# A mixture of experts whose token rows are gathered instead of scattered, in a decoder kernel on one core

## The chip, the core and the metric

The kernel runs on one core of a Trainium2 chip. The core has a matrix engine (PE), a vector engine (DVE), a scalar engine (ACT), GpSimd (POOL) and a queue engine (SP) that mostly issues DMAs. Each runs its own list of instructions and waits on semaphores that the others raise. On-chip memory (SBUF) has 128 partitions; PE writes to PSUM, which has 8 banks. The metric is the device time of one execution in microseconds, lower is better.

## What is computed

x is 16 blocks of 128 tokens by 256 features, in float32. The decoder is six stages, each adding its result to x: two of layer 0 (a recurrent mixing, then a grouped attention), a feed-forward stage with experts, and three of layer 1 (windowed attention, cross attention, a gated feed-forward). The change is about the third, which is, cut to what matters:

```python
x = x + ffn(_layernorm(x))

def ffn(h):
    dense = _rms((_gelu_tanh(_rms(h, pre1) @ w_gate) * (_rms(h, pre1) @ w_up)) @ w_down, post1)
    probs = softmax(_rms(h) * router_scale * ROOT @ router_w)        # 8 experts
    top_w, top_i = top_k(probs, 2)
    top_w = top_w / sum(top_w) * per_expert_scale[top_i]
    moe = sum over the 2 chosen e of top_w * ((_gelu_tanh(m @ we_gate[e]) * (m @ we_up[e])) @ we_down[e])
                                             # m = _rms(h, pre2)
    return _rms(dense + _rms(moe, post2), post)
```

## The kernel before

The third stage (function `experts`, L1059 to L1830) starts when all engines have left the second (`gqa`). Its tokens are 4 groups of 4 blocks (`GB` = 4, `NG` = 4).

**The normalised tokens y.** DVE aggregates the statistics of all 16 blocks (`aggregate`, L195), POOL makes one factor per token from them (L200 to L1232, first for 4 blocks, then for 12), and DVE multiplies (`normalise`, L1591: 4 blocks, then 12).

**PE's opening.** `turn(0)` and `turn_ahead(1..3)` transpose y, 8 matmuls of 128x128 for each group (L1281, L1292); ACT copies the result to SBUF; `route(g)` multiplies it by the router's weights (L1300, 8 matmuls with 8 columns, which the trace prints as 16). `turn(0)`, `turn_ahead(1)` and `route(0)` come first, then the first dense step, `gate_up(0,0)`, and behind it the other turns and routes.

**The dense part.** Every group has 8 steps. A step is `gate_up(g,q)` (L1333, 12 matmuls of 512 columns) and, one step late, `down(g,q-1)` (L1350, 12 matmuls of 256 columns). Between the two ACT takes the gelu (L1552), DVE multiplies (`ex_gated`, L1675), ACT rounds to the high part (`ex_hidden_high`, L1559) and DVE makes the low part (L1682). `down` waits for the high part. Each operand is split in two parts, so that three matmuls make one product; the weights' low parts are made on POOL (L1237).

**Where each token goes.** Once all four routes are done, DVE reads the logits, ACT takes the exponent, and DVE ranks the experts of each token by comparing all pairs (L1606 to L1616, tiles of 128x1024). A token's two experts are the ones with rank under 2. `count()` on PE (L1308 to L1311, before `gate_up(0,4)`) counts how many tokens of each expert come before each one. From that DVE finds for each token two slots (`ex_index`) among 40 tiles of 128 slots, each tile of a single expert (`ex_owner`).

**The rows by slot.** POOL scatters the rows of y into the DRAM tensor `slot_x` by 32 indirect DMAs (L1244), which wait for the slots of all tokens. SP then fetches the 40 tiles in 20 pairs (L1181), into 4 buffers. Slots that no token fills have to hold zeros: SP writes the whole of `slot_x` in the first stage (L276, 5 MB).

**The mixture.** It comes on PE between dense groups 1 and 2 (`EARLY` = 2). A pair of tiles is turned (L1362), goes through its expert's gate and up (L1376), the hidden is turned (L1386) and goes through the expert's down (L1396). SP stores its result to `slot_y`. When all 20 pairs are stored, POOL gathers for each block the two rows of every token into `ex_first` and `ex_second` (L1220, 32 indirect DMAs). Right after the last store SP loads the fourth stage's weights wk, wv, wo (L182).

**The late work.** Beside dense groups 2 and 3 (16 steps, n = 0 to 15) and behind them, four groups of results are put together: ACT weighs `ex_first` (`weigh_first`, L1484), DVE adds the weighed `ex_second` (`mix`, L1704), ACT squares (L1468), POOL makes the norm (`normalise`, L1214 and L1215), DVE scales and adds the dense part (L1711, L1723), ACT squares again, POOL makes the norm, DVE scales (L1729), adds to x (`add_sum`, L1736) and takes the statistics (`measure`, L1741). Each group starts 4 steps behind the one before it (`late`, `late_step`, `FIRST_LATE` = 2). The fourth stage's first matmul needs the statistics of all of x.

## Time and profile before

| | us |
|---|---|
| median of 3 runs | 1493.51 (1492.75 to 1494.72) |
| the profiled execution | 1493.66, of which its span is 1491.6 |
| first stage / second stage | 0 to 205 / 205 to 343 |
| third stage | 344.4 to 646.6 |
| its dense groups 0 and 1 end, its mixture starts and ends, groups 2 and 3 end | 459.3, 480.0, 547.1, 628.2 |
| fourth, fifth and sixth stage | from 646.6 to the end |
| mean granted clock of PE | 0.936 of full speed |

Times inside the trace count from the start of the span. The row of a group of instructions gives its start, its busy time, the engine, the line, the operation, what it writes and reads, how many instructions of what shape, and in brackets how long the engine sat idle before it and who ended that.

### The profile page before, as it was taken

What the parts mean: (1) busy time and instruction counts of PE and PEld (TensorE: products, weight loads), DVE (VectorE), ACT (ScalarE), POOL (GpSimd) and SP (SyncE); (2) the same over time, 40 slices, a digit from 0 to 9 for tenths busy, and PEclk for the clock granted to TensorE, in tenths of its full rate; (3) what the DMA queues carried; (4) which work ended last, traced back from release to release, by engine and by line L of the source; (5) the groups of instructions that cost most, each with busy time, mean ns of one, the idle gap of its engine ahead of it and who ended that gap; (6) DMA issues with size and microseconds to landing.
All of it is one profiled execution on the core that took longest, in us unless ns stands there. A gap on an engine that the chain in (4) does not pass through costs nothing. (4 is left out here: it accounts for less than half of the span.)

```text
span 1491.6 us, 26479 instructions
## 1 busy us (share of the span) xinstructions
PE 1249.2 (84%) x7839; PEld 983.0 (66%) x7886; DVE 981.7 (66%) x1905; ACT 843.0 (57%) x2174; POOL 641.1 (43%) x724
## 2 busy tenths in 40 slices
PE   6994889995793999638998998899896888879998
PEld 4673555554683897526777777777774555548887
DVE  5998788883453544797778778777773566643443
ACT  5443899993452555545666666666662555543322
POOL 2003666663436015457667666666663333320000
PEclk9996999997797999958999999999998999988999
DMA  8400433310003454120000000000000000000000
GB/s 312 156 0 14 105 93 84 84 43 1 0 33 116 142 195 138 29 102 1 2 1 0 0 0 0 0 0 0 0 1 3 4 4 3 3 1 1 15 14 29
DMA packets 49684, 64.52 MB, mean 43 GB/s; under 512 B 6032, under 2 KB 42896, under 8 KB 48336
## 3 DMA queue, kind: packets, MB, share of 16 engines
q1 hardware_dynamic: 46544, 55.27, 11.8%
q0 software_dynamic: 3072, 8.39, 1.7%
q8 instruction: 37, 0.61, 0.2%
q14 instruction: 31, 0.25, 0.1%
HBM read 38.48 MB, written 16.78 MB: 37 GB/s over the span
## 5 line engine op out<-in xcount | busy, mean ns | idle before, releaser
L2209 ACT ACTIVATE wi_weights<-wi_psum,wi_bias,wi_scale 128x128 f32<-128x128 f32 x256 | 113.7, 454 | 118.2 <-DVE wi_bias L2319 118.2
L929 ACT ACTIVATE gq_weights<-gq_psum,gq_least 128x128 f32<-128x128 f32 x512 | 151.2, 524 | 2.0 <-DVE gq_least L977 2.0
L1984 POOL TENSOR_TENSOR wi_straight<-wi_straight,wi_crossed 128x512 f32<-128x512 f32 x80 | 103.3, 1291 | 10.9 <-DVE wi_crossed L2305 10.8
L977 DVE TENSOR_REDUCE gq_least<-gq_psum 128x4 f32<-128x512 f32 x128 | 86.1, 686 | 26.9 <-PE gq_psum L854 25.5
L1972 POOL TENSOR_TENSOR wi_scratch<-wi_sums,wi_eps 128x4 f32<-128x4 f32 x80 | 35.1, 438 | 132.6 <-DVE wi_sums L2288 131.2
L1973 POOL TENSOR_TENSOR wi_scale<-wi_scratch,minus_half 128x4 f32<-128x4 f32 x80 | 84.6, 1058 | 6.3
L2108 PE MATMUL wi_psum<-wi_weights_t,wi_values 128*128 128x512 f32 x128 | 68.9, 620 | 20.6 <-DVE wi_weights_t L2326 20.6
L2310 DVE TENSOR_REDUCE wi_top<-wi_psum 128x4 f32<-128x512 f32 x64 | 44.0, 687 | 63.1 <-PE wi_psum L2099 63.1
L2099 PE MATMUL wi_psum<-wi_k_t,wi_q_t 128*128 128x128 f32 x512 | 67.5, 275 | 19.8 <-ACT wi_q_t L2200 18.7
L862 PE MATMUL gq_psum<-const,gq_weights 128*128 128x128 f32 x512 | 79.1, 278 | 1.3 <-ACT gq_weights_t L937 0.3
L2735 DVE TENSOR_REDUCE cr_top<-cr_psum 128x4 f32<-128x512 f32 x64 | 43.7, 682 | 46.0 <-PE cr_psum L2550 46.0
L862 PEld LDWEIGHTS gq_psum<-const,gq_weights 128*128 128x128 f32 x512 | 63.1, 142 | 14.8 <-DVE gq_weights_t L990 4.2
L1994 POOL TENSOR_TENSOR wi_weights<-wi_weights,wi_inverse 128x512 f32<-128x512 f32 x64 | 66.2, 1034 | 9.5 <-remote 5.1
L2099 PEld LDWEIGHTS wi_psum<-wi_k_t,wi_q_t 128*128 128x128 f32 x512 | 67.9, 193 | 1.6
L2050 PEld LDWEIGHTS wi_psum<-const,wi_straight 128*128 128x128 f32 x320 | 39.6, 143 | 42.7 <-issue 41.8
L2490 POOL TENSOR_TENSOR cr_keys_diagonal<-cr_qk,const 128x256 f32<-128x256 f32 x32 | 19.4, 626 | 112.0 <-ACT cr_qk L2662 112.0
L854 PE MATMUL gq_psum<-gq_keys_diagonal,gq_h_t 128*128 128x512 f32 x128 | 63.8, 503 | 3.7 <-ACT gq_weights L929 3.7
L2305 DVE TENSOR_TENSOR wi_crossed<-wi_raw,wi_sin_q 128x256 f32<-128x256 f32 x128 | 64.9, 547 | 0.0
L2303 DVE TENSOR_TENSOR wi_straight<-wi_raw,wi_cos_q 128x512 f32<-128x512 f32 x64 | 61.0, 953 | 0.0
L2928 DVE TENSOR_TENSOR ff_gated<-ff_gated,ff_psum 128x512 f32<-128x512 f32 x32 | 22.0, 688 | 58.3 <-PE ff_psum L2848 58.0
L2181 ACT ACTIVATE wi_raw<-wi_psum 128x512 f32<-128x512 f32 x80 | 48.3, 603 | 20.7 <-PE wi_psum L2086 20.2
L2326 DVE COPY wi_weights_t<-wi_psum 128x512 f32<-128x512 f32 x64 | 43.8, 684 | 21.8 <-PE wi_psum L2064 21.6
(384 smaller groups left out, 3890.0 us busy)
## 6 DMA issues: line engine op xcount, KB each, us to landing
gq_keys<-in_ctx_keys_dram SPq DMA_DIRECT2D x16, 512.0 KB, 3.8
gq_keys_diagonal<-gq_key_parts SPq DMA_DIRECT2D x64, 128.0 KB, 3.9
slot_x<-rw_zero SPq DMA_DIRECT2D x1, 5120.0 KB, 18.0
ex_slot_rows<-slot_x SPq DMA_DIRECT2D x20, 256.0 KB, 3.0
slot_y<-ex_s_out SPq DMA_DIRECT2D x20, 256.0 KB, 2.2
x<-in_x_dram SPq DMA_DIRECT2D x4, 512.0 KB, 8.8
gate<-in_gate_dram SPq DMA_DIRECT2D x2, 1024.0 KB, 5.3
up<-in_up_dram SPq DMA_DIRECT2D x2, 1024.0 KB, 7.5
```

What stands on the lines that cost most here:

```text
L854: pe.matmul(ps[:, u % 4, :], h_t[:, s, u, :], kbd[s][:, u, :, :], start=True, stop=True).then_inc(scored, 1)
L862: mm = pe.transpose(ps[:, bank(unit, t, u), j * P:j * P + P], weights[:, u % RINGS, j * P:j * P + P], ident)
L929: e = act.activation(weights[:, u % RINGS, j * P:j * P + P], ps[:, u % 4, j * P:j * P + P], ACT.Exp, bias=least[:, u % 4, j:j + 1], scale= ...
L977: dve.tensor_reduce(least[:, u % 4, :], rows(u), AX.X, ALU.min).then_inc(topped, 1)
L1973: found = pool.tensor_tensor(scale[:, scale_at], scratch2[:], net.half[:, 0:4], ALU.pow)
L1984: added_up = pool.tensor_tensor(straight[:, at], straight[:, at], crossed[:, at], ALU.add)
L1994: pool.tensor_tensor(weights[:, g % 2], weights[:, g % 2], wide(inverse[:, g % 2], [P, 4, P]), ALU.mult).then_inc(normalised, 1)
L2099: mm = pe.matmul(bank[:, j * P:j * P + P], q_t[:, g % 2, j, :], k_t[:, s, g, :], start=False, stop=(j == 3), skip_group_check=True)
L2108: pe.matmul(ps[:, AV, :], values[:, s, g * DH:g * DH + DH], weights_t[:, g % 2], start=True, stop=True).then_inc(attended, 1)
L2209: act.activation(weights[:, g % 2, j, :], ps[:, SC + g % 2, j * P:j * P + P], ACT.Exp, bias=bias[:, g % 2, j:j + 1], scale=scale[:, g, j:j ...
L2303: dve.tensor_tensor(straight[:, at], raw[:, at], over_heads(cos[:]), ALU.mult).then_inc(parts, 1)
L2305: dve.tensor_tensor(crossed[:, at, :, to], raw[:, at, :, source], over_heads(sin[:, to]), ALU.mult).then_inc(parts, 1)
```

## The change

- **y early.** y gets a place of its own (`ffn_y`) that the second stage can already write. In its last iteration DVE aggregates blocks 0 to 11 (after x of these is final), POOL makes their factors (`ffn_norm_scale`, 12 columns) and DVE normalises blocks 0 to 5 in its tail. POOL's folding of norm weights into the stage's weights (`fold_ffn0`, 4 instructions per half) is cut in two, the first half ahead of an addition to x. In the third stage DVE aggregates 4 blocks, normalises 6 to 11, and 12 to 15 after POOL's 4 columns.
- **PE's opening.** All four turns and routes come before `gate_up(0,0)`; ACT takes the exponent before the first gelu; `count()` comes behind `gate_up(0,2)`.
- **Two experts by maximum.** DVE finds the largest probability, takes 2 off it and finds the largest again (`choose`), on tiles of 128x128, instead of comparing all pairs.
- **Gathers in place of scatters.** SP writes y to the DRAM tensor `ffn_rows` in order of tokens (2 DMAs). DVE builds, spread over the steps of groups 0 and 1, tables that say in which tile and at which place in it each token stands (`find_blocks`, `find_far`, `spread_far`, `spread_near`); PE multiplies them (`find_tokens`, 32 matmuls of 80 columns in bf16) to the list of tokens of each tile (`ex_token`). POOL gathers each pair of tiles from `ffn_rows` with 2 indirect DMAs, 40 in all, the first four pairs (8 DMAs) ahead of the mixture, and each later one when its buffer is free. The zeroing of `slot_x` falls away, since an empty slot names token 0, whose result no one reads.
- **The late work is placed anew** over the 16 steps; POOL, not DVE, adds the sums of groups 0 and 1 to x, and the last group is worked in two pairs of blocks.
- **The fourth stage's wk, wv, wo** are loaded after all of POOL's last gathers have landed. The semaphores of the stage are cleared by SP in the fourth.

On PE at the start of the stage, first before, then in the change (ffn_y is y, ex_h_t the turned tokens, router_w the router's weights):

```order
L1281 MATMUL ex_psum<-const,ex_y 128x128 x8
L1292 MATMUL ex_psum<-const,ex_y 128x128 x8
L1300 MATMUL ex_psum<-router_w,ex_h_t 128x8 x8
L1333 MATMUL ex_psum<-ex_h_high,ex_gate_high 128x512 x2
...
L1333 MATMUL ex_psum<-ex_h_low,ex_up_high 128x512 x2
L1300 MATMUL ex_psum<-router_w,ex_h_t 128x8 x8
L1292 MATMUL ex_psum<-const,ex_y 128x128 x8
L1300 MATMUL ex_psum<-router_w,ex_h_t 128x8 x8
L1292 MATMUL ex_psum<-const,ex_y 128x128 x8
L1300 MATMUL ex_psum<-router_w,ex_h_t 128x8 x8
L1350 MATMUL ex_psum<-ex_down_high,ex_hidden_high 128x256 x4
```

```order
L1320 MATMUL ex_psum<-const,ffn_y 128x128 x8
L1330 MATMUL ex_psum<-const,ffn_y 128x128 x8
L1338 MATMUL ex_psum<-router_w,ex_h_t 128x8 x8
L1330 MATMUL ex_psum<-const,ffn_y 128x128 x8
L1338 MATMUL ex_psum<-router_w,ex_h_t 128x8 x8
L1330 MATMUL ex_psum<-const,ffn_y 128x128 x8
L1338 MATMUL ex_psum<-router_w,ex_h_t 128x8 x16
L1382 MATMUL ex_psum<-ex_h_high,ex_gate_high 128x512 x2
```

The first dense matmuls moved behind the last three routes and two of the turns.

On POOL from the last low parts of the weights to the first gathers of results, before and in the change:

```order
L1237 TENSOR_TENSOR ex_down_low<-down,ex_down_high 128x256
L1214 TENSOR_TENSOR ex_scratch<-ex_squares,ex_eps 128x4
L1215 TENSOR_TENSOR ex_norm<-ex_scratch,minus_half 128x4
L1244 DMA slot_x<-ex_y,ex_index 5120x256 x32
L1214 TENSOR_TENSOR ex_scratch<-ex_squares,ex_eps 128x4
L1215 TENSOR_TENSOR ex_norm<-ex_scratch,minus_half 128x4
L1220 DMA ex_first<-slot_y,ex_index 128x256
```

```order
L1269 TENSOR_TENSOR ex_down_low<-down,ex_down_high 128x256
L1245 DMA ex_slot_rows<-ffn_rows,ex_token 128x256 x8
L1239 TENSOR_TENSOR ex_scratch<-ex_squares,ex_eps 128x4
L1240 TENSOR_TENSOR ex_norm<-ex_scratch,minus_half 128x4
L1239 TENSOR_TENSOR ex_scratch<-ex_squares,ex_eps 128x4
L1240 TENSOR_TENSOR ex_norm<-ex_scratch,minus_half 128x4
L1245 DMA ex_slot_rows<-ffn_rows,ex_token 128x256 x32
L1259 DMA ex_first<-slot_y,ex_index 128x256
```

The 32 scatters ahead of the mixture became 8 gathers ahead of it and 32 inside it.

On ACT over steps n = 8 to 11 (the first half of dense group 3), where the squares and the weighing stand between the gelus, before and in the change:

```order
L1552 ACTIVATE ex_gated<-ex_psum 128x512
L1559 ACTIVATE ex_hidden_high<-ex_gated 128x512
L1468 ACTIVATE ex_junk,ex_squares<-ex_dense 128x256 x4
L1468 ACTIVATE ex_junk,ex_squares<-ex_first 128x256 x4
...
L1484 ACTIVATE ex_first<-ex_first,ex_weight 128x256 x4
...
L1468 ACTIVATE ex_junk,ex_squares<-ex_first 128x256 x4
```

```order
L1603 ACTIVATE ex_gated<-ex_psum 128x512
L1607 ACTIVATE ex_hidden_high<-ex_gated 128x512
L1515 ACTIVATE ex_junk,ex_squares<-ex_first 128x256 x8
...
L1531 ACTIVATE ex_first<-ex_first,ex_weight 128x256 x4
...
L1515 ACTIVATE ex_junk,ex_squares<-ex_first 128x256 x4
L1515 ACTIVATE ex_junk,ex_squares<-ex_dense 128x256 x4
...
L1515 ACTIVATE ex_junk,ex_squares<-ex_first 128x256 x4
```

Five sets of four squares stand in these four steps where three stood.

The core of the diff:

```diff
@@ gqa: POOL @@
+                if last:
+                    fold_ffn0(pool, net, 0)
                 if not (isinstance(t, int) and t < 2):
                     add(t - 2)
-            fold_ffn0(pool, net)
+            fold_ffn0(pool, net, 1)
+            pool.wait_ge(aggregated_ffn, NB - GB)
+            ffn_norm_scale(pool, own, net, scratch, scratch2, slice(0, NB - GB)).then_inc(rstd_ffn, 1)
             add(NB - 2)
             add(NB - 1)
@@ experts: SP @@
-            sp.wait_ge(owned, 1)
-            sp.wait_ge(scattered, 16 * TOP * NB)
-            for k in range(XINS + 3):
-                fetch(k)
+            sp.wait_ge(normed, NB - GB - DONE)
+            sp.dma_start(rows[:, 0:NB - GB, :], y[:, 0:NB - GB, :]).then_inc(rows_out, 16)
+            sp.wait_ge(normed, NB - DONE)
+            sp.dma_start(rows[:, NB - GB:NB, :], y[:, NB - GB:NB, :]).then_inc(rows_out, 16)
             for k in range(PAIRS):
                 store(k)
+            for g in range(NG):
+                sp.wait_ge(gathered[g], 16 * TOP * GB)
             load_attn1(nc, net, ("wk", "wv", "wo"))
@@ experts: POOL @@
+            def fetch(k):
+                for j in range(2):
+                    pool.indirect_dma_start(slot_rows[:, k % XINS, j, :], None, net.ffn_rows[:],
+                                            bass.IndirectOffsetOnAxis(ap=token[:, 2 * k + j:2 * k + j + 1], axis=0)
+                                            ).then_inc(slots_in[k % XINS], 16)
-            for i in range(TOP):
-                pool.wait_ge(indexed, i + 1)
-                for b in range(NB):
-                    pool.indirect_dma_start(net.slot_x[:], bass.IndirectOffsetOnAxis(ap=index[i][:, b:b + 1], axis=0),
-                                            y[:, b, :], None).then_inc(scattered, 16)
+            pool.wait_ge(spread, 4)
+            for k in range(XINS):
+                fetch(k)
+            for g in range(EARLY):
+                normalise(GB * g, GB * g + GB, 0)
+            for k in range(XINS, PAIRS):
+                pool.wait_ge(s_turned, k - XINS + 1)
+                fetch(k)
             gather(0, 8)
-            normalise(0, 1)
-            gather(8, 10)
-            normalise(0, 2)
-            gather(10, 12)
+            normalise(0, 4, 1)
+            gather(8, 11)
+            normalise(0, 4, 2)
+            gather(11, 12)
@@ experts: ACT @@
             def late(n):
+                for g, at in enumerate((3, 6, 9, 12)):
+                    if n == at:
+                        weigh_first(g)
+                    if n == at + 2:
+                        square_mixture(g)
+                for g, at in enumerate((8, 10, 15)):
+                    if n == at:
+                        square_sum(GB * g, GB * g + GB)
+                if n == STEPS + 2:
+                    square_dense(EARLY)
@@ experts: DVE, a table @@
+            def find_blocks():
+                link(dve.tensor_scalar(block_of[:], place[:], 1.0 / P, None, ALU.mult))
+                shape = [P, TOP, NB, TILES]
+                link(dve.tensor_tensor(far[:], wide(block_of[:], shape),
+                                       iota[:, 0:TILES].unsqueeze(1).unsqueeze(1).broadcast_to(shape), ALU.is_ge))
+                link(dve.tensor_reduce(block_of[:], far[:], AX.X, ALU.add))
```

## Rows read from the trace of the kernel before

**Rows 1.** Waits of PE over the third stage: us in total, times, longest us.

```profile
PE ex_psum L1362 <- issue: 22.8, 2, 20.7
PE ex_psum L1350 <- ACT ex_hidden_high L1559: 8.3, 6, 3.1
PE ex_psum L1281 <- DVE ex_y L1591: 7.7, 1, 7.7
PE ex_psum L1308 <- DVE ex_running L1624: 6.7, 1, 6.7
```

**Rows 2.** Timeline of PE, opening: start us, us, engine, line, operation, count, idle before.

```profile
357.79 1.97 PE L1292 MATMUL ex_psum<-const,ex_y 128*128 128x128 f32 x8 [5.94 <-DVE ex_y L1591]
359.55 3.42 PE L1300 MATMUL ex_psum<-router_w,ex_h_t 128*128 128x8 f32 x16
362.82 1.20 PE L1333 MATMUL ex_psum<-ex_h_high,ex_gate_high 128*128 128x512 f32 x2
...
367.82 1.85 PE L1300 MATMUL ex_psum<-router_w,ex_h_t 128*128 128x8 f32 x16
369.52 1.07 PE L1292 MATMUL ex_psum<-const,ex_y 128*128 128x128 f32 x8
...
382.17 1.05 PE L1333 MATMUL ex_psum<-ex_h_high,ex_gate_high 128*128 128x512 f32 x2
```

**Rows 3.** Windows: us, busy (x) of PE, PEld, DVE, ACT, POOL; granted clock.

```profile
348.00:366.00 18.00, 10.18 (x40) 9.11 (x41) 9.03 (x18) 4.67 (x8) 10.33 (x16) 0.50 0.00 0
368.00:374.00 6.00, 4.83 (x43) 4.59 (x44) 0.69 (x1) 1.09 (x2) 0.00 (x0) 1.00 0.01 3
374.00:384.00 10.00, 8.82 (x39) 8.04 (x38) 1.18 (x3) 6.31 (x12) 4.21 (x6) 0.51 0.00 0
395.00:475.00 80.00, 56.67 (x322) 49.45 (x322) 39.62 (x76) 31.06 (x67) 40.12 (x42) 0.88 0.14 50
```

**Rows 4.** Timeline of PE, first turns of the pairs 0, 8 and 12.

```profile
480.00 1.09 PE L1362 MATMUL ex_psum<-const,ex_slot_rows 128*128 128x128 f32 x4 [20.69 <-issue]
...
504.85 0.60 PE L1362 MATMUL ex_psum<-const,ex_slot_rows 128*128 128x128 f32 x4
...
517.36 0.60 PE L1362 MATMUL ex_psum<-const,ex_slot_rows 128*128 128x128 f32 x4
```

**Rows 5.** Timeline of DVE, first blocks of y.

```profile
348.44 1.38 DVE L1591 TENSOR_SCALAR ex_y<-x,mean_var,rstd 128x256 f32<-128x256 f32 x4 [2.85 <-POOL rstd L1232]
```

**Rows 6.** Timeline of DVE, ranking the experts.

```profile
388.29 1.76 DVE L1606 TENSOR_TENSOR ex_above<-ex_prob 128x1024 f32<-128x1024 f32 x1
...
399.21 1.21 DVE L1616 TENSOR_REDUCE ex_rank<-ex_above 128x128 f32<-128x1024 f32 x1
400.46 0.28 DVE L1617 TENSOR_SCALAR ex_chosen<-ex_rank 128x128 f32<-128x128 f32 x1
```

**Rows 7.** Lines on POOL: ns min/median/max, starts, landing; last a DMA issue.

```profile
L1244 POOL DMA_INDIRECT slot_x<-ex_y,ex_index x32: 956/960/1346, 434.1 to 474.7; - x32
...
L1220 POOL DMA_INDIRECT ex_second<-slot_y,ex_index x16: 946/959/1424, 552.3 to 610.2; - x16
...
DMA to landing us min/median/max: 2.7/2.9/8.6
...
L1237 POOL TENSOR_TENSOR ex_up_low<-up,ex_up_high x8: 716/754/1716, 355.4 to 409.6; 128x256 fp32r<-128x256 f32 x8
...
slot_x<-rw_zero SPq DMA_DIRECT2D x1, 5120.0 KB, 18.0
```

**Rows 8.** Timeline of ACT and DVE, late work and its end.

```profile
564.10 1.71 ACT L1484 ACTIVATE ex_first<-ex_first,ex_weight 128x256 f32<-128x256 f32 x4 [5.69 <-DMA ex_second<-slot_y,ex_index]
...
638.47 0.42 ACT L1468 ACTIVATE ex_junk<-ex_first 128x256 f32<-128x256 f32 x1 [6.20 <-DVE ex_first L1723]
...
640.41 0.19 ACT L1468 ACTIVATION_READ_ACCUMULATOR ex_junk<-ex_first 128x1 f32 x1
...
641.99 1.67 DVE L1729 SCALAR_TENSOR_TENSOR ex_first<-ex_first,ex_norm,rows 128x256 f32<-128x256 f32 x4 [0.78 <-POOL ex_norm L1215]
```

497 lines of the change are left out of this document (291 added, 206 removed).

## The prediction

> **What bounds the kernel now.** I read the waits of PE over the third stage first, since PE is the engine that everything there hands its work to. Its one large wait is for the first turned slots of the mixture, 20.7 us in one piece; then come 8.3 us in six pieces for the high part of the hidden, 7.7 us for the first blocks of y, and 6.7 us ahead of the count [rows 1]. The timeline of PE gives the places: turns, routes and the first dense step are interleaved, and the second `gate_up` starts only at 382.17 [rows 2]. The clock shows why that opening is dear: PE is granted 0.50 of full speed (its level of 1.2 GHz) from 348 to 366 and about that again from 374 to 384, with routes and turns at full clock between [rows 3]. The mixture itself runs at an even pitch [rows 4]. ACT, DVE and POOL bound nothing in dense groups 0 and 1 by their sums. In groups 2 and 3 the order on ACT does, and behind the last matmul DVE does.
>
> **The opening.** Before, `turn(0)` stands 7.65 us behind PE's readiness for y, and `turn_ahead(1)` 5.94 us, both for DVE's normalising; `gate_up(0,0)` starts at 362.82 [rows 1, 2]. In the change blocks 0 to 5 are done in the second stage, so `turn(0)` can start at the stage's start, about 344.6. The last four blocks need POOL's four columns and DVE's 1.38 us, which the row of before has over at 349.8 [rows 5]; that hides behind the first turns. PE then has four turns and four routes. At the low clock a turn takes 1.76 us from start to start (357.79 to 359.55) and a route 3.27 (359.55 to 362.82), so 4 x 5.03 = 20.1 and the end at 364.7. At full clock a turn is 1.07 and a route 1.70 [rows 2], so 11.1 and 355.7; there ACT binds, which has copies and roundings of weights up to about 357. The first piece is likely at full clock, since the second stage ends at it, so I take 363.5. `gate_up(0,0)` is 5.1 us at the low clock (362.82 to 367.9), so the second one starts at 368.6 and not at 382.17. Before, `down(0,0)` was done by then, which costs 1.4 at full clock: 382.2 - 368.6 - 1.4 = **12.2 us won**.
>
> The count waited 6.7 us [rows 1]. DVE's way there was four instructions on 128x1024 of 1.76 us and one more of 1.2; choosing by maximum is twelve of at most 128x128, for which the marking of the chosen, 0.28 us, is the nearest row [rows 6]: 3.5 us, done near 375.5, while PE reaches `count()` behind `gate_up(0,2)` at about 374.5. One or two us of wait remain: **5.2 won**, and 1 more because no long wait leaves the next matmuls slow, as one does at 480.00, where a turn's four take 1.09 us instead of 0.60 [rows 4]. `find_tokens` adds 32 matmuls of 80 columns in bf16. By columns alone a float32r matmul of 512 columns took 0.23 us, so 80 columns 0.04; as dear as a routed matmul it would be 1.70 / 8 = 0.21 [rows 2]. So 1.3 to 6.8 us; I take 2.6, nearer to the lower end, as these are one pass each. Sum for dense groups 0 and 1: -12.2 - 5.2 - 1.0 + 2.6 = -15.8, so **-16**, and they end at 443.3, not 459.3.
>
> DVE's new tables hide in those steps. A step of dense work is 4.18 us on PE, of which DVE has 1.4 for itself. The largest piece, `find_blocks`, is two instructions on 128x1280 and four small ones: 1.5 each by the reduction's 1.21 for 1024 elements, 2.2 by the compare's 1.76, which shared the time with POOL's work [rows 6]. With its own 1.4 the step is 5 to 6.5 us, and PE has about 1.5 us of slack before it waits for the next high part. So 0 to 1 us of stall here and the same in two other steps: 0 to 3 us, of which 1 is in the rounding above.
>
> **The idle time before the mixture.** The 20.69 us up to 480.00 are empty because the 32 scatters run from 434 to 475.6 at a pitch of 1.26 us, POOL being in line behind its other work, and SP's fetches follow [rows 1, 4, 7]. In the change `read_tokens` is done behind the fourth step of group 1, near 425; eight gathers at 1.26 us end by 435, and the first pair lands 2.9 us after its second issue, near 430.5. The mixture wants it at 443. **-20.7 us**, with a margin of 12 us: were the tables, the scatters' price or the landing that much worse, nothing would change.
>
> **The mixture.** It took 67.1 us. Its steady part is 12.51 us for four pairs (504.85 to 517.36) and stays [rows 4]; what goes is the low clock of its first 7 us, about 2.4 us of half-speed work, while the latency of the first pair stays. POOL now issues two gathers per pair: 2 x 1.26 = 2.52 us against a mean pair of 3.13, so POOL is 80% busy but not the bound, and each gather is issued when a buffer frees, four pairs (12.5 us) ahead of its use, for which 2.52 + 2.9 are needed. But `normalise(4,8,0)`, which waits for ACT's squares of group 1, stands ahead of the fifth pair on POOL: squares 2.1 us, norm 1.2, gathers and landing 5.4, so it lands near 452.5, when PE, 11 us into the mixture, wants it. 0 to 1 us. So **-1.5**.
>
> **Dense groups 2 and 3** took 81.1 us (547.1 to 628.2) for 16 x 4.18 = 66.9 and two turns. 5.7 us of ACT's wait for gathered rows, in the step that weighs group 0 [rows 8], go: the weighing moves to n = 3, 12 us on, and the loads of wk, wv, wo no longer run beside the gathers, which then landed in up to 8.6 us [rows 7]. That gives back 4 us. What comes: a set of four squares is 2.1 us (638.47 to 640.6) and the weighing 1.7 [rows 8]. In n = 8 to 11 ACT has five sets, one weighing and four times a gelu and a high part of 0.6 each with 0.7 us between for DVE: 10.5 + 1.7 + 7.6 = 19.8 us against 4 x 4.18 = 16.7. And `gather(11,12)` stands behind `normalise(0,4,2)` on POOL, which waits for the squares of n = 8, so `weigh_first(2)` at n = 9 starts 1.2 + 2.5 + 2.9 = 6.6 us behind them and not 4.2 or less. Together that is 3.1 + 2.4 to 5 us, with a high part late by each set's length: I take 8. The waits of before in that part of ACT's order, 0.6 + 0.6 + 0.3 and some, move. The net is -4 + 8 = **+4** (from 0 to +8).
>
> **The tail** is 18.4 us now. Working the last group in pairs lets the last leg (scale, add to x, statistics, from 641.99 to 646.6 [rows 8]) run for two blocks instead of four behind the last norm, 2.3 us, and squares of two blocks instead of four, 1.1: **-3.4** (-2 to -4). POOL's two additions of 128x1024 stand between norms: `norm` of the last group waits at most one of them, which is hidden by DVE's work on group 2.
>
> **Priced at nothing.** The zeroing of `slot_x` is a transfer of the first stage that nobody waits for. The 12 factors, 6 us on POOL, stand ahead of the last two additions to x in a stretch where POOL waits for DVE; if they were late, the second stage would end up to 2 us later. The fourth stage's 5 MB are issued when all gathers have landed, near 575 by my account; as many bytes of zeros took 18.0 us to land [rows 7], and that stage starts near 608, so 15 us are to spare.
>
> **Sum** against the profiled execution: 1493.66 - 16 - 20.7 - 1.5 + 4 - 3.4 = **1456 us**. That execution is within 0.15 us of the median, so no more is to be shifted.
>
> **A rule that speaks against the change.** The POOL rows of before carry 32 indirect DMAs of 956 to 1346 ns, median 960, in a stretch where DVE is busy half the time [rows 3, 7]: DVE hardly moves them. The Trainium skill, "SBUF — State Buffer", section "Who interferes with whom", says that GpSimd cannot write a DMA's descriptors while DVE runs a mode with two ports, and gives some 3100 ns for one that takes 620 alone; by that page's figure, as an estimate, 32 gathers inside the mixture would take 32 x 3.4 = 109 us where it has 66, and the sum would be near 1500. The trace of before shows nothing of that size, so the sum does not take it; the first rival below is the mechanism, priced by rows.
>
> **Rivals.**
>
> *POOL's gathers bound the mixture.* The pair needs 3.13 us on PE, so from 1.57 us per gather on POOL is the bound. The dearest indirect DMA of before is 1.35 + 0.30 = 1.65 us: 66 us for 40, the same as the mixture. An elementwise POOL instruction shared with DVE has gone from 0.75 to 1.72 [rows 7]; each gather stretched by as much is 2.23, 4.5 per pair, so 89 us and 24 more: 1480. Slower than before it becomes only from 1.57 + 37.7 / 40 = 2.5 us for each gather, twice the row. For it: DVE is busy half of the mixture. Against: the 32 rows.
>
> *The opening at full clock.* The turns and routes start when the second stage's matmuls have just ended, and routes were at 1.00 from 368 to 374 [rows 3]. Then `gate_up(0,0)` starts at 357 and takes 2.9: -8.7, 1447. Against: the same kinds of work fell to 0.50 at 374 while they ran. The Trainium skill, "TensorE: Matmul & The Clock Gate", Part 4, holds that transposes don't count as busy for the clock; by that the opening would stay low to its end, as I have it.
>
> *The order of ACT and DVE costs more.* The stalls in groups 2 and 3 at 12 instead of 8 and the tables' at 3 or 4: +6 to +12, 1462 to 1468.
>
> *The token list comes late.* If it takes 12 us more than I count, pairs are late one by one: up to 10 us of the 20.7 come back, 1466. It needs several tables to be doubled.
>
> *The change doesn't start y early:* were the factors late, the 7.7 and 5.9 us would return in part, 1462.
>
> **How the numbers follow.** Forecast and its neighbourhood (1450 to 1461): 0.56. Opening at full clock, 1443 to 1450: 0.14. Costlier order or late y or list, 1462 to 1470: 0.22. Gathers stretched but still faster, 1471 to 1489: 0.05. Slower than before by the gathers: 0.02, and 0.01 for the same. The range 1443 to 1470 leaves out 8 in 100; narrower it would cut into the bounds of the late work. A measurement of this kernel tells a change from none by about 0.2%, 3 us: faster 0.97, same 0.01, slower 0.02.
>
> **What would show it.** PE's first turn near 344.6 and second `gate_up` near 369; the wait ahead of the count under 2 us; no wait at the mixture's start and its first turn near 443; gathers at 1.26 us pitch and pairs at 2.80 and 4.11; waits for the high part of 8 us or so in group 3, with ACT idle for `ex_second` at n = 9; from last `down` to last statistics 15 us. The forecast is wrong if gathers run over 1.6 us, if the clock is 1.00 before 360, or if PE waits for h or high parts in groups 0 and 1 by over 3 us.

## The result

The changed kernel takes 1454.95 us (median of 4 runs, 1453.96 to 1456.42), and the kernel before 1493.74 us on the same chip: a ratio of 0.974 (95% interval 0.9729 to 0.9752), 2.6% faster. The profiled execution took 1456.42 us, of which its span is 1454.3, against 1493.66 and 1491.6. The forecast was 1456, the range 1443 to 1470.

All of the difference lies in the third stage. PE is through with the second stage at 342.2 us before and at 342.1 now, so what was moved into that stage and what fell away in the first made no difference that shows (between the traces of the kernels below that moment varies by 2 us). The fourth stage's first matmul came at 649.25 us and now comes at 611.71; behind it both spans have the same 842 us.

| us | before | after | moved by | forecast |
|---|---|---|---|---|
| first turn starts | 349.88 | 344.26 | | |
| second `gate_up` starts | 382.17 | 364.86 | | |
| dense groups 0 and 1 end | 459.31 | 438.03 | -21.3 | -16 |
| idle until the mixture | 20.7 | 0 | -20.7 | -20.7 |
| mixture, to the next `gate_up` | 67.1 | 67.8 | +0.7 | -1.5 |
| dense groups 2 and 3 | 81.1 | 86.6 | +5.5 | +4 |
| last matmul to DVE's last statistics | 18.4 | 14.9 | -3.5 | -3.4 |
| from there to the fourth stage's first matmul | 2.7 | 4.6 | +1.9 | 0 |
| sum | | | -37.4 | -37.6 |

The first view is the timeline of PE of the changed kernel, its opening (start, time, engine, line, operation, count, idle before). It answers to [rows 2].

```profile
344.26 1.06 PE L1320 MATMUL ex_psum<-const,ffn_y 128*128 128x128 f32 x8 [2.19 <-PEq L720]
345.32 1.09 PE L1330 MATMUL ex_psum<-const,ffn_y 128*128 128x128 f32 x8
...
348.32 1.07 PE L1330 MATMUL ex_psum<-const,ffn_y 128*128 128x128 f32 x8
...
351.81 1.97 PE L1330 MATMUL ex_psum<-const,ffn_y 128*128 128x128 f32 x8 [0.24 <-DVE ffn_y L1081]
...
360.26 1.20 PE L1382 MATMUL ex_psum<-ex_h_high,ex_gate_high 128*128 128x512 f32 x2
...
364.86 0.63 PE L1382 MATMUL ex_psum<-ex_h_high,ex_gate_high 128*128 128x512 f32 x2
```

PE waits 0.24 us for y, and the second `gate_up` (364.86) directly follows the first. A turn takes 1.07 to 1.09 us at 345 and 348 and 1.97 at 351.81: the clock. The windows of the changed kernel (as in [rows 3], the granted clock is the third number from the end) say when:

```profile
348.00:350.00 2.00, 2.00 (x21) 2.00 (x20) 1.67 (x3) 1.89 (x6) 1.84 (x5) 1.00 1.03 346
...
352.00:354.00 2.00, 2.00 (x11) 2.00 (x10) 0.00 (x0) 0.18 (x1) 2.00 (x4) 0.50 0.68 231
354.00:360.00 6.00, 6.00 (x30) 6.00 (x30) 0.00 (x0) 1.82 (x5) 3.18 (x5) 0.50 0.05 17
360.00:364.00 4.00, 4.00 (x11) 3.23 (x12) 0.58 (x2) 2.19 (x3) 0.00 (x0) 0.50 0.00 0
364.00:366.00 2.00, 2.00 (x10) 1.63 (x9) 0.88 (x2) 0.15 (x1) 0.00 (x0) 0.99 0.00 0
```

Full clock (2.4 GHz) up to 350, half (1.2 GHz) from 352 to 364, though PE was busy all but 0.24 us of the time, and full again 4 us into the first dense step. The Trainium skill, "TensorE: Matmul & The Clock Gate", Part 4, says of transposes that the full clock doesn't engage for them, since they don't count as busy in the same way. That fits a clock that falls under turns and tiny matmuls and rises under dense ones; no run here tells turns from routes.

The waits of PE over the stage, for [rows 1] (us in total, times, longest):

```profile
PE ex_psum L1397 <- ACT ex_hidden_high L1607: 12.6, 5, 4.4
PE ex_psum L1423 <- DVE ex_s_low L1873: 3.7, 2, 2.1
...
PE ex_psum L1409 <- issue: 1.4, 1, 1.4
PE ex_psum L1346 <- DVE ex_running L1672: 1.2, 1, 1.2
```

The 20.7 us and the 7.7 us of before are gone, the 6.7 us have become 1.2. What has grown is the wait for the high part, 8.3 to 12.6, and that for the slots' low part, `ex_s_low`: 3.7 us in two waits, where the same view of before has one of 1.7.

The tokens' list and the gathers for [rows 4] and [rows 7]; first PE's timeline:

```profile
416.19 1.32 PE L1359 MATMUL ex_psum<-ex_far_parts,ex_near 128*128 128x80 bf16 x32
...
437.87 0.60 PE L1409 MATMUL ex_psum<-const,ex_slot_rows 128*128 128x128 f32 x4
...
442.68 0.79 PE L1423 MATMUL ex_psum<-ex_egu_high,ex_s_high 128*128 x2 [2.14 <-DVE ex_s_low L1873]
```

The first gather in POOL's timeline:

```profile
423.07 1.21 POOL L1245 DMA_INDIRECT ex_slot_rows<-ffn_rows,ex_token  x1 [39.39 <-DVE ex_token L1744]
```

The group of all gathers (count, then min, median and longest in ns, and from when to when):

```profile
L1245 POOL DMA_INDIRECT ex_slot_rows<-ffn_rows,ex_token x40: 945/949/1308, 423.1 to 487.8; - x40
```

The 32 matmuls of the list took 1.32 us in all. The first gather is issued at 423.07, 15 us before PE turns the first pair at 437.87. The 40 gathers took 945 to 1308 ns, median 949, in a stretch (423 to 488) in which DVE was busy 38.1 of 65 us.

The late work in the timelines of four engines, for [rows 8]; PE:

```profile
559.67 1.23 PE L1397 MATMUL ex_psum<-ex_down_high,ex_hidden_high 128*128 128x256 f32 x4 [3.42 <-ACT ex_hidden_high L1607]
...
579.51 1.23 PE L1397 MATMUL ex_psum<-ex_down_high,ex_hidden_high 128*128 128x256 f32 x4 [4.41 <-ACT ex_hidden_high L1607]
```

ACT:

```profile
556.05 1.70 ACT L1531 ACTIVATE ex_first<-ex_first,ex_weight 128x256 f32<-128x256 f32 x4 [4.29 <-DMA ex_second<-slot_y,ex_index]
```

DVE:

```profile
572.68 3.81 DVE L1794 SCALAR_TENSOR_TENSOR ex_first<-ex_first,ex_norm,rows 128x256 f32<-128x256 f32 x4 [2.50 <-POOL ex_norm L1240]
```

POOL:

```profile
572.63 2.39 POOL L1252 TENSOR_TENSOR x<-x,ex_first 128x1024 f32<-128x1024 f32 x1
```

The late work of step n stands behind that step's high part on ACT, and so holds up the one of step n + 1; the waits of PE are named here by the n of the late work. Two things are to be seen. ACT waits 4.29 us at n = 9 for the rows of block 11. And DVE's scaling of four blocks at 572.68, 1.67 us elsewhere, takes 3.81 us; it begins 0.05 us behind POOL's addition of 128x1024, which takes 2.39.

Not all of what groups 2 and 3 lost is waiting. Both kernels have the same 394 matmuls there. In the windows of that stretch (547.14 to 628.22 before, 505.66 to 592.23 now) PE is busy 71.9 us before and 74.7 now, and idle 9.2 and 11.9; the granted clock is 0.97 and 0.92. So 2.7 us of the 5.5 are idle time, and 2.8 are matmuls at the lower clock, as the 1.23 us for four behind each of the two long waits above (0.74 behind a short one).

The stage's end: DVE's last statistics, and what follows, in the timelines; DVE:

```profile
606.39 0.75 DVE L1825 BATCH_NORM_STATS2 stats<-x 128x6 f32<-128x256 f32 x2
610.01 1.17 DVE L195 BATCH_NORM_AGGREGATE mean_var<-stats 128x2 f32<-128x6 f32 x16 [2.86 <-PEq L1091]
```

POOL:

```profile
602.94 0.82 POOL L1240 TENSOR_TENSOR ex_norm<-ex_scratch,minus_half 128x2 f32<-128x2 f32 x1
609.97 0.10 POOL L2085 MEMSET wi_eps<- 128x4 f32 x1 [6.21 <-POOLq L1091]
```

DVE is done at 607.14 and the fourth stage starts at 610. POOL's last norm ended at 603.76, and POOL too is ready only 6.21 us behind it.

### The profile page after: what moved, and what is told of

It reads as the page before. It is cut to its first block and busy times, and to the rows that moved or that the text cites. A ratio compares the mean times of both kernels' runs of the same rounds, so it can differ in the third digit from the quotient of the medians.

```text
span 1454.3 us, 26646 instructions
## 1 busy us (share of the span) xinstructions
PE 1255.8 (86%) x7918; PEld 982.7 (68%) x7918; DVE 989.9 (68%) x1910; ACT 841.6 (58%) x2172; POOL 652.3 (45%) x737
## 3 DMA queue, kind: packets, MB, share of 16 engines
q1 hardware_dynamic: 38048, 46.90, 10.5%
## 5 line engine op out<-in xcount | busy, mean ns | idle before, releaser
L2231 PE MATMUL wi_psum<-wi_weights_t,wi_values 128*128 128x512 f32 x128 | 68.8, 619 | 20.5 <-DVE wi_weights_t L2449 20.5
L2222 PEld LDWEIGHTS wi_psum<-wi_k_t,wi_q_t 128*128 128x128 f32 x512 | 67.8, 193 | 1.7
L1245 POOL DMA_INDIRECT ex_slot_rows<-ffn_rows,ex_token x40 | 38.8, 970 | 57.2 <-DVE ex_token L1744 39.4
## 6 DMA issues: line engine op xcount, KB each, us to landing
down<-in_down_dram SPq DMA_DIRECT2D x2, 1024.0 KB, 10.1
```

The source lines that it names most:

```text
L2222: mm = pe.matmul(bank[:, j * P:j * P + P], q_t[:, g % 2, j, :], k_t[:, s, g, :], start=False, stop=(j == 3), skip_group_check=True)
L2231: pe.matmul(ps[:, AV, :], values[:, s, g * DH:g * DH + DH], weights_t[:, g % 2], start=True, stop=True).then_inc(attended, 1)
```

## The experiments

Twelve kernels were run, edits of the changed kernel and combinations of them; each was timed in 5 rounds against the kernel before. Ratios are to the kernel before; the changed kernel's is 0.9740, and a difference in time is that of the ratios unless medians are named. An interval is about 0.0013 to either side unless given, 2 us, so effects of 1 or 2 us are read from the traces and not from the times. The edits are shown shortened, with comments added. No run takes the gathers out again, or the search by maximum: that the 20.7 us went by the gathers is read from the traces, and the runs below test what could have stood in their way.

### y begun only in the third stage

```diff
-            ffn_norm_scale(pool, own, net, scratch, scratch2, slice(0, NB - GB)).then_inc(rstd_ffn, 1)
-                normalise_ffn(dve, net, b)          # blocks 0 to 5, in gqa
-    DONE = 6
+    DONE = 0
+            ffn_norm_scale(pool, own, net, scratch, scratch2, slice(0, GB)).then_inc(rstd_ready, 1)
+            ffn_norm_scale(pool, own, net, scratch, scratch2, slice(GB, NB)).then_inc(rstd_ready, 1)
```

> The change with y not begun in the second stage: statistics, factors (4 columns, then 12) and all 16 blocks of y come in the third stage, as before the change; the order of turns and routes, the tables, the gathers and the late work stay. Theory (the early y is what shortens the opening): the first turn comes near 349.9 instead of 344.3 and the second turn near 357.8; with three turns and four routes at the low clock behind it and a first dense step the second gate_up starts near 381 instead of 364.9, so the whole is slower than the changed kernel by 12 to 16 us (1467 to 1471). Rival (the new order of PE and ACT, with one loading of the exponent's table, is what paid, and y is hidden): slower by 0 to 6 us (1455 to 1461).

Measured: 1471.34 us, ratio 0.9852 (0.9836 to 0.9867), 17 us slower than the changed kernel (16.4 by the medians), a little more than expected. PE's timeline of this kernel:

```profile
350.75 1.97 PE L1310 MATMUL ex_psum<-const,ffn_y 128*128 128x128 f32 x8 [8.44 <-DVE ffn_y L1071]
358.25 1.97 PE L1320 MATMUL ex_psum<-const,ffn_y 128*128 128x128 f32 x8 [5.53 <-DVE ffn_y L1071]
360.01 3.42 PE L1328 MATMUL ex_psum<-router_w,ex_h_t 128*128 128x8 f32 x16
...
376.73 1.20 PE L1372 MATMUL ex_psum<-ex_h_high,ex_gate_high 128*128 128x512 f32 x2
...
381.78 0.63 PE L1372 MATMUL ex_psum<-ex_h_high,ex_gate_high 128*128 128x512 f32 x2
```

Both waits of before are back (8.4 and 5.5 us), and behind them all turns and routes run at the slow clock. The second `gate_up` comes at 381.78, 16.9 us later than in the change, where before it came at 382.17. So the new order of PE alone won nothing here; the early y is worth nearly the whole of the opening's gain. PE idles 11.5 us less (2.2 and 0.2 against 8.4 and 5.5), and the other 5.4 us are the work up to 350 and behind 364 at full clock, where this kernel has 0.50 from 350 to 381.

### A third gather per pair

```diff
+                if k >= XINS:
+                    pool.indirect_dma_start(gated[:, (k % XINS) // 2, (k % 2) * D:(k % 2) * D + D], None,
+                                            net.ffn_rows[:], ...).then_inc(slots_in[k % XINS], 16)
```

> The changed kernel with a third, unused gather for each of the pairs 4 to 19 in the mixture, so POOL issues 3 x 1.25 = 3.76 us of work per pair against a mean pair of 3.13 on PE. Theory (POOL binds the mixture from 1.57 us per gather on, and two at 1.25 leave 0.6 us per pair free): PE waits for the rows of each pair, and the mixture grows from 67.8 to 76 us, so 8 us slower than the changed kernel (1463). Rival (the buffers' four pairs of lead absorb it, or something else sets the pitch of the mixture): under 2 us. Rival (gathers are slowed by DVE or by one another once they stand back to back): over 12 us.

Measured: 1465.48 us, ratio 0.9818 (0.9804 to 0.9831), 11.7 us slower (10.5 by the medians). In its trace the mixture takes 78.3 us and not 67.8, 10.5 us more, where 8 were expected; what the 8 left out is at least in part the clock, which is lower here. One stretch in the windows, first of the changed kernel (stretch, its length, then busy time and instructions of PE, PE's weight load, DVE, ACT and POOL, granted clock, DMA share and GB/s):

```profile
445.00:500.00 55.00, 50.55 (x422) 49.62 (x422) 28.78 (x61) 30.17 (x69) 28.59 (x31) 0.99 0.55 149
```

A third gather per pair:

```profile
445.00:500.00 55.00, 46.19 (x346) 44.64 (x346) 24.54 (x53) 25.59 (x58) 41.59 (x45) 0.90 0.59 165
```

POOL is busy 41.6 of 55 us where it was 28.6, PE 46.2 where it was 50.6, and the granted clock is 0.90 and not 0.99. So POOL binds the mixture at three gathers, 3.76 us per pair, and not at two. The rival of the prediction that could have made the change slower has its mechanism right, and its price nearly: (3.76 - 3.13) x 16 pairs is 10.1 us. Only its condition, gathers of over 1.57 us, isn't met.

### The list two steps later

```diff
-                    if g == EARLY - 1 and q == 3:
+                    if g == EARLY - 1 and q == 5:
                         find_tokens()
-                    if g == EARLY - 1 and q == 3:
+                    if g == EARLY - 1 and q == 5:
                         read_tokens()
```

> The changed kernel with the list of tokens made two steps later (PE's 32 matmuls and DVE's reading behind the sixth step of group 1), so the first gather is issued near 431.5 and not at 423.1. Theory (the fetching has over 8 us of margin): the first pair lands near 437.5, when PE wants it at 437.9, the second when it wants it at 439.9, and the norm and the fifth pair follow the eighth gather near 442: under 1 us slower than the changed kernel. Rival (what is ahead of the mixture is short already, and each us of delay costs one): 5 to 8 us slower (1460 to 1463).

Measured: 1454.46 us, ratio 0.9749 (0.9736 to 0.9763). The first gather is issued at 428.6, 5.5 us later, and the mixture starts without a wait, as in the changed kernel, and takes 69.0 us, 1.2 more, with the clock still at 0.65 from 446 to 448, where it was 1.00. The margin took up nearly all of the delay; the 20.7 us are won with room, but not with 12 us of it.

### The late work: one gather's place, and who adds to x

The first edit puts all gathers of group 2 ahead of the norm of group 0's sum:

```diff
-            gather(8, 11)
-            normalise(0, 4, 2)
-            gather(11, 12)
+            gather(8, 12)
+            normalise(0, 4, 2)
```

> The changed kernel with one edit on POOL: all gathers of group 2 (blocks 8 to 11) stand ahead of the norm of group 0's sum, none behind it. Theory (ACT's wait of 4.3 us for ex_second in step n = 9 comes from the gathers of block 11 queued behind that norm, which waits for the squares of n = 8): that wait goes, PE's wait of 3.4 us for the high part falls to about 1, and the whole is 2 to 3 us faster (1452 to 1453). Rival (ACT's squares alone bind steps 8 to 11, and the wait overlaps them): under 0.5 us.

Measured: 1450.38 us, ratio 0.9721 (0.9708 to 0.9734). PE's wait of 3.4 us at n = 9 falls to 0.8, and groups 2 and 3 take 84.0 us and not 86.6. As expected, 2.6 us; behind it one of 1.5 us comes at n = 10, and the one at n = 12 is 5.3 and not 4.4.

The second takes the addition of groups 0 and 1 from POOL and gives it to DVE:

```diff
-            add_sum(0)                              # POOL, 128x1024
-            add_sum(1)
+                    add_sum(0, 4)                   # DVE, 4 of 128x256, at n = 11
+                    add_sum(4, 8)                   # at n = 15
```

> The changed kernel with the sums of groups 0 and 1 added to x by DVE (4 instructions of 128x256 each, in steps n = 11 and n = 15) and not by POOL. Theory (POOL's addition of 128x1024 holds DVE up: in the trace DVE's scaling of four blocks took 3.81 us instead of 1.67 beside the first, a low part 1.62 instead of 0.69 beside the second): DVE gets back 3.1 us and does 2.9 more, in steps with room; PE's wait for the high part of 4.4 us falls to about 2.4, and the whole is 1 to 2 us faster (1453 to 1454). Rival (POOL's additions are free): DVE has 2.9 us more to do, most of it in the step before the tail, and the whole is 1 to 2 us slower (1456 to 1457).

Measured: 1451.59 us, ratio 0.9727 (0.9713 to 0.974). In the trace groups 2 and 3 take 83.3 us and not 86.6, and DVE's part of the tail 16.7 and not 14.9: 3.3 won, 1.8 lost, 1.5 us net. POOL's two additions held DVE up by 2.1 us and by 0.9. PE's wait of 4.4 us at n = 12 falls to 2.3, so the addition was half of it. In the other half DVE waits for POOL's norm (2.50 us in the changed kernel, 1.36 here) and scales the dense part (1.67 us) ahead of the product that the high part needs. The Trainium skill, "SBUF — State Buffer", section "Who interferes with whom", says that a DVE instruction with two SBUF inputs contends with a GpSimd instruction that reads SBUF, and that whoever comes first has the port for the whole instruction; here DVE, 0.05 us behind, lost 2.14 us of the 2.34 that POOL still had to go.

### The mixture's start

```diff
             normalise(0, GB, 0)                     # POOL
             for k in range(XINS, PAIRS):
+                if k == XINS + 3:
+                    normalise(GB, 2 * GB, 0)
-                    square_dense(EARLY - 1)         # ACT, ahead of the mixture
+                    if i == 0:                      # in its fourth turn
+                        square_dense(EARLY - 1)
```

> The changed kernel with the squares of dense group 1 on ACT moved from ahead of the mixture into its fourth turn, and the norm that waits for them on POOL moved behind the gathers of the seventh pair. Theory (ACT's squares hold up the first pair's high part, and the norm on POOL holds up the fifth pair's gathers): PE's waits of 2.14 us at 442.7 and of 1.54 us at 452.7 fall to about 0.5 and 0, the clock does not fall at 442, and the mixture takes 63 to 65 us instead of 67.8: 3 to 5 us faster than the changed kernel. Rival (the first wait is the latency of turn, rounding and splitting itself): 0 to 1.5 us.

Measured: 1450.8 us, ratio 0.972 (0.9707 to 0.9733). The wait for `ex_s_low` at 442.7 is gone, and the clock holds there. That of 1.4 us ahead of it stays, and so does that of 1.5 us at 452.7, expected to go: it stands at 448.0 with 1.59 us, so POOL's norm was not its cause. The mixture takes 66.6 us, only 1.2 less, since a new wait of 1.9 us stands at the eighth pair (461.4), behind which the clock falls to 0.50: POOL now stands 3.80 us before the norm until ACT's squares are done, and the eighth pair's gathers are behind it. By time it is 3 us faster, by trace 1.2; 3 to 5 were expected. PE's timeline of the changed kernel around the fifth pair's turn:

```profile
450.57 0.60 PE L1409 MATMUL ex_psum<-const,ex_slot_rows 128*128 128x128 f32 x4
452.71 0.51 PE L1423 MATMUL ex_psum<-ex_egu_high,ex_s_high 128*128 x2 [1.54 <-DVE ex_s_low L1873]
```

PE's timeline of this kernel:

```profile
448.01 0.53 PE L1424 MATMUL ex_psum<-ex_egu_high,ex_s_high 128*128 x2 [1.59 <-issue]
...
461.36 0.51 PE L1424 MATMUL ex_psum<-ex_egu_high,ex_s_high 128*128 x2 [1.88 <-DVE ex_s_low L1875]
```

### A drain of POOL before the end

```diff
             add_sum(0)
+            pool.drain()
```

> The changed kernel with one more instruction: a drain of POOL's queue behind its first addition to x, in a stretch where POOL has nothing to do. Theory (what separates the third stage from the fourth is POOL: at the stage's end its drain takes some 0.08 us for each indirect DMA of the stage, 5.56 us behind its last instruction with 64 of them, 6.21 with 72, 7.51 with 88, so that DVE, long done, waits 2.86 us): with the queue drained before, POOL is through at once, the fourth stage's first statistics follow DVE's last by 0.3 to 1 us, and the whole is 2 to 2.5 us faster than the changed kernel (1452.5). Rival (the 5 to 7 us are a fixed cost of leaving so long a program on POOL, or of the queue at that moment): the gap stays 2.86 and the time is the same or 0 to 1 us slower.

Measured: 1451.92 us, ratio 0.9728 (0.9715 to 0.9742). This kernel at the stage's end, in the timelines; DVE:

```profile
606.89 1.17 DVE L195 BATCH_NORM_AGGREGATE mean_var<-stats 128x2 f32<-128x6 f32 x16 [0.32 <-PEq L1091]
```

POOL:

```profile
606.86 0.10 POOL L2086 MEMSET wi_eps<- 128x4 f32 x1 [3.67 <-POOLq L1091]
```

The gap behind DVE's last statistics is 0.32 us where it was 2.87, 2.5 us as expected; the ratio says 1.8, within its interval. What POOL still needs behind its last instruction when the stage ends, against the indirect DMAs of the stage (the view of the waits at that place):

| kernel | indirect DMAs | POOL's last instruction to the next stage | gap behind DVE |
|---|---|---|---|
| before | 64 | 5.56 | 0.97 |
| changed | 72 | 6.21 | 2.87 |
| three gathers | 88 | 7.51 | 4.17 |
| changed, drained before | 72 | 3.67, waiting for DVE | 0.32 |

Each DMA adds 0.081 us: (7.51 - 6.21) / 16, and (6.21 - 5.56) / 8. So the fourth stage began where POOL's last norm and this drain allowed, and by the trace before the change too (no run drains that kernel early); the eight DMAs more and the shorter tail on DVE made it visible.

### The weights' load, and the place of the first dense step

The load of wk, wv, wo as before the change, at the mixture's end:

```diff
-            for g in range(NG):
-                sp.wait_ge(gathered[g], 16 * TOP * GB)
             load_attn1(nc, net, ("wk", "wv", "wo"))
```

> The changed kernel with the fourth stage's wk, wv, wo loaded when the mixture's results are stored, as before the change, and not when the last gather has landed. Theory (the load's 4.5 MB stand in the gathers' way: beside it one took 8.6 us to land, against 3.8 in the change, but the weighing of group 0 has moved from n = 0 to n = 3): the first gathers land late, up to 8 us, ACT's wait of 0.5 us at n = 3 becomes 1 to 3, PE has slack there, and the whole is 0 to 1 us slower. Rival (the gathers are not touched, and the weights for the fourth stage were on the edge of being late): the same or up to 1 us faster.

Measured: 1454.51 us, ratio 0.9749 (0.9736 to 0.9762). As expected, gathered rows land later (at most 8.6 us and not 3.8), and ACT's wait for them at n = 3 is 1.92 us and not 0.48. PE has slack there: one wait of 0.5 us in group 2 is all that is seen of it, and the time is the same. The new place costs nothing either: issued at 571.9 to 573.2, the last of the four landed 13.3 us later, and the stage starts at 610.

The first dense step ahead of the last two turns (one of these uses another PSUM bank for it, and waits for the first group's tokens to be split):

```diff
             turn_ahead(1)
             route(0)
+            gate_up(0, 0)
             turn_ahead(2)
             route(1)
```

> The changed kernel with the first dense step of PE put between route(0) and turn_ahead(2), as before the change; y stays early and the exponent still precedes the first gelu. PE's work is the same. Theory (turns and routes alone do not hold the clock, a dense step gives it back: it fell to 0.50 at 351 and came back only 4 us into the first dense step): the step stands at 348 to 353, keeps or restores full clock for some microseconds of the routes behind it, and the second gate_up starts 1 to 3 us earlier than 364.9, as does all else. Rival (where the slow stretch lies does not matter, it lasts as long): within 0.7 us; the gelu of the first step comes late and PE waits for it up to 1 us more.

Measured: 1455.48 us, ratio 0.9746 (0.9733 to 0.976). The dense step starts at 349.39 behind a wait of 2.45 us for its weights' low part from POOL, with the clock fallen; the clock is back at 1.00 from 356 to 362, and down again for the second `gate_up`, which waits 0.8 us for the logits' reader. PE's timeline:

```profile
349.39 1.22 PE L1384 MATMUL ex_psum<-ex_h_high,ex_gate_high 128*128 128x512 f32 x2 [2.45 <-POOL ex_down_low L1269]
...
363.02 1.19 PE L1384 MATMUL ex_psum<-ex_h_high,ex_gate_high 128*128 128x512 f32 x2 [0.80 <-DVE ex_prob L1642]
```

Its windows:

```profile
350.00:352.00 2.00, 2.00 (x6) 1.61 (x5) 0.25 (x4) 0.00 (x0) 1.50 (x3) 0.50 0.70 240
...
360.00:362.00 2.00, 2.00 (x20) 2.00 (x20) 0.00 (x0) 0.78 (x3) 1.75 (x3) 1.00 0.00 0
364.00:366.00 2.00, 2.00 (x6) 1.60 (x5) 0.84 (x2) 1.24 (x3) 0.00 (x0) 0.50 0.00 0
```

It starts at 363.02 and in the change at 364.86, but this trace's first turn too is 1.5 us earlier (342.75 against 344.26), and group 1 ends at 438.10 against 438.03, so from its own start this kernel is 1.6 us slower up to there. The clock does come back behind the dense step, and holds for 6 us of turns and routes, but the slow stretch only moves.

### All that helped, together

The four edits (x on DVE, gather ahead, mixture's start, drain) in one kernel:

> The edits of x_on_dve, gather_ahead, mix_start and early_drain together on the changed kernel. Alone they gave ratios to the kernel before of 0.9727, 0.9721, 0.9720 and 0.9728 against 0.9740 of the changed kernel. Theory (each removes a wait of its own place): the gains add up to 0.0064, so a ratio near 0.9676, 1445 us. Rival (the two edits of the late work remove the same wait, since in each ACT's and DVE's load in steps 8 to 15 is what is left): 0.969 to 0.971, 1447 to 1450 us.

Measured: 1447.75 us (1443.18 to 1449.91), ratio 0.9684 (0.9668 to 0.9699), between the two forecasts, 0.9676 and 0.969 to 0.971. In the trace groups 2 and 3 take 82.1 us; the mixture takes 68.8 here and not 66.6: its new wait at the eighth pair is 2.6 us, and behind it the clock is 0.50 up to 470.

With the squares of dense group 2 later, its norm on POOL behind all gathers, and the gathers of blocks 12 and 13 earlier:

```diff
-                if n == STEPS + 2:                  # ACT: square_dense(EARLY)
+                if n == 13:
-                if n == 12:                         # DVE: scale_dense of blocks 8 to 11
+                if n == 14:
```

> The kernel of the four edits with the squares of dense group 2 on ACT moved from step n = 10 to n = 13, its scaling on DVE from n = 12 to n = 14, its norm on POOL behind all gathers, and the gathers of blocks 12 and 13 ahead of the norm of group 0's sum. Theory (five sets of squares in steps 8 to 11 are one too many, and PE's waits there are ACT's): PE's waits for the high part in steps 9 to 14 fall from some 7 us to 3, and it is 2 to 4 us faster than the four edits alone. Rival (the work only moves, and the waits of the last two steps grow by as much): within 1 us of it.

Measured: 1442.98 us, ratio 0.9661 (0.9648 to 0.9675). Groups 2 and 3 take 78.6 us, 3.5 less than with the four edits, and their waits for the high part fall from 9.8 us in all to 6.6. All but the first and the last of them fall from 6.1 together to 1.6, and the one at n = 12 is gone; the one in the last step grows from 2.9 to 4.5, so a part of the work has only moved, as the rival had it.

With the norm of dense group 1 one pair later on POOL (`if k == XINS + 4`):

> The replanned kernel with the norm of dense group 1 on POOL one pair later, behind the gathers of the eighth pair and not the seventh. Theory (in the replanned kernel POOL stands 3.8 us before that norm, waiting for ACT's squares, and the rows of the eighth pair then reach PE late, its wait of 2.2 us at 462.5 with a fall of the clock): the norm finds its squares done, POOL doesn't stand, PE's wait goes, and the mixture takes 64 to 65 us instead of 66.9: 2 to 3 us faster, near 1440.5. Rival (that wait is the ordinary one at every fourth pair, where PE loads the experts' numbers, 1 us in the steady part, and only its clock differed): under 1 us.

Measured: 1440.29 us (1437.61 to 1440.56), ratio 0.9627 (0.9587 to 0.9667; the kernel before scattered more in that comparison, so the medians say more: 2.7 us under the one above). The mixture takes 64.2 us. The timelines of its middle; POOL:

```profile
448.19 0.20 POOL L1239 TENSOR_TENSOR ex_scratch<-ex_squares,ex_eps 128x4 f32<-128x4 f32 x1 [1.28 <-ACT ex_junk L1514]
```

PE:

```profile
447.48 0.53 PE L1422 MATMUL ex_psum<-ex_egu_high,ex_s_high 128*128 x2 [1.59 <-issue]
...
459.99 0.51 PE L1422 MATMUL ex_psum<-ex_egu_high,ex_s_high 128*128 x2 [1.03 <-issue]
```

POOL stands 1.28 us before the norm and not 3.80, and PE's waits in the mixture are down to 0.9 to 1.6 us each, the ones at every fourth pair among them. It is the fastest of all, by the medians 14.7 us under the changed kernel and 3.6% under the kernel before.

## Why the prediction was right

**The idle time before the mixture** (-20.7) came as worked out: scatters ahead of the mixture became gathers inside it that POOL has time for. The margin was put at 12 us, within which "nothing would change". The list was read at 422 and not 425, and the run with the list 5.5 us later lost 1.2 us, so the margin is large, but smaller than that.

**The opening and groups 0 and 1** came out 5.3 us better than -16. Two terms were too dear. The clock: I took nearly all of the opening at the slow level, 363.5 and 368.6, but the clock held to 350 and came back during the first dense step, 360.26 and 364.86; 3.7 us of the 5.3. That is nearly half of the 8.7 us of the rival "the opening at full clock", which I gave 14 in 100, and one of my signs of a wrong forecast, a clock of 1.00 before 360, was there from 344 to 350. `find_tokens` was put at 2.6 and took 1.32: as there was no row of one-pass matmuls, the bounds were 1.3 to 6.8, and the truth lies at the lower one. The stalls by DVE's new work came about as allowed for (0 to 3 us): 1.6 us at 400 by the tables and 1.0 at 369.7 by the search by maximum. The price of `find_blocks` (two of 1.5 us) was right.

**The mixture** was to win 1.5 us and lost 0.7. The step that failed is "what goes is the low clock of its first 7 us": there was no longer an idle time to pull the clock down, but PE waited 1.4 and 2.1 us at once, the second because ACT squared dense group 1 first, and the clock fell all the same (0.64 from 442 to 444, 0.51 to 446). I had seen the same squares in POOL's way, for the fifth pair (0 to 1 us), and not in ACT's. For the fifth pair they cost nothing: its turn at 450.57 follows without a wait, and the 1.5 us behind it stay when the squares move. The run that moved them shows the wait of 2.1 gone, the one of 1.4 is in every run, and the final kernel has 64.2 us.

**Groups 2 and 3** (+5.5, forecast +4) went as argued at n = 8 to 11: ACT waited 4.3 us for block 11 and PE 3.4; taking the gather out of line gave 2.6 back. The second part, 4.4 us at n = 12, was not in the forecast. There ACT waits for DVE, and DVE is late by POOL's addition to x (2.1 us), POOL's norm and the scaling of the dense part; giving the addition to DVE left 2.3 us, and placing that scaling and its squares later as well (the replanned kernel) left none. Half of the 5.5 is matmuls at a lower clock, which the forecast didn't price.

**The tail**: DVE's part is 3.5 us shorter, by the pairs of blocks, as worked out. But of POOL's two additions the forecast had only that a norm waits for one of them, "which is hidden by DVE's work on group 2". That DVE itself waits for them it did not have: the first addition held DVE for 2.1 us in group 3, the second for 0.9. And 1.9 us went at the stage's end to POOL's drain, which I did not have at all; the row that would have shown it, POOL idle for 5.56 us at the end of the stage in the kernel before, looked like waiting for DVE.

**The rival on the other side**, gathers that bind the mixture, was rejected on the 32 rows of [rows 7], and rightly: 40 gathers at a median of 949 ns with DVE busy 38.1 of 65 us. The Trainium skill, "SBUF — State Buffer", section "Who interferes with whom", has the rule on descriptors and DVE's modes with two ports (the figure of 3100 ns stands in its section "A bandwidth-pool intuition that's wrong", and is for a DVE copy). No run here shows which mode DVE's instructions ran; if one in the mixture ran such a mode, it cost a gather at most the 0.36 us between 949 and 1308 ns.

So the sum was right to 2 us for one good reason, the large terms, and for one of luck: the gain was put 5.3 us too low in the opening, and 2.2, 1.5 and 1.9 us too high in the mixture, in groups 2 and 3 and at the stage's end, and these cancel.

## What to carry to other kernels

A scatter that must be complete before anyone may read stands on the path with all its instructions; a gather per consumer spreads the same instructions over the time that they are used in, and was free here as long as (instructions per item) x (pitch of one on the issuing queue) stayed under the consumer's time per item: 2 x 1.25 us against 3.13 cost nothing, 3 x 1.25 cost 10.5 us. Work that everyone waits for at a stage's start, here y, is best put in the gaps of the stage before; here the idle time that it removed also decided at what clock the next work ran. After such a change, read again what shares a queue with the new instructions: the further 14.7 us lay in where a few groups of small instructions stood on ACT, DVE and POOL.

## What the runs showed of the hardware

- What POOL needed between its last instruction and the next stage grew by 0.081 us for each indirect DMA of the stage (5.56, 6.21 and 7.51 us for 64, 72 and 88), and a drain issued earlier, where POOL was idle, took it off the end (gap 2.87 to 0.32 us).
- An addition of 128x1024 on POOL (2.39 us) held up DVE instructions with two inputs in SBUF for nearly its whole rest: four such took 3.81 us in place of 1.67, one 1.62 in place of 0.69.
- Indirect DMAs at a pitch of 1.25 us were hardly slowed by DVE at work (38.1 of 65 us): median 949 ns, at most 1308.
- Under turns and routes PE's clock fell though PE was busy nearly all the time (1.00 until 350, 0.50 from 352), and it came back 4 us into the dense matmuls. Behind a dense step it held for 6 us of turns and routes (356 to 362, with the first dense step put ahead).
- 32 matmuls of 80 columns in bf16 took 1.32 us together.
